# A cross-attention and mixture-of-experts block on one core: the second linear's ReLU values pass from ScalarE to VectorE as 16-bit integers instead of 32-bit floats

## What is computed

```python
def bitnet_linear(x, W, b):
    w_scale = jnp.maximum(jnp.mean(jnp.abs(W)), 1e-05)
    qW = jnp.sign(W) * (jnp.abs(W) > 0.5 * w_scale).astype(W.dtype)
    i_scale = jnp.maximum(jnp.max(jnp.abs(x)), 1e-08) / 127.0
    qx = jnp.clip(jnp.round(x / i_scale), -128.0, 127.0)
    out = jnp.einsum('...i,oi->...o', qx, qW) * (w_scale * i_scale)
    return out + b
...
h = jax.nn.relu(bitnet_linear(concatenated, W_f1, b_f1))   # 8192 tokens x 512
return bitnet_linear(h, W_f2, b_f2)                        # h is rounded to 0..127 first
```

## Time and profile before

| what | value |
|---|---|
| median of 3 runs | 553.0 us (550.98, 553.0, 557.37) |
| the profiled execution's own time | 551.12 us |
| its span in the trace | 549.3 us |
| busy over the span | PE 70%, DVE 69%, ACT 65%, POOL 36% |
| chain that ended last, by engine | PE 30%, DVE 24%, ACT 15%, issue 14%, POOL 13%, DMA 3% |
| line L759 (the ReLUs) in that chain | 2% as `xqT`, 2% as `tok_b` |

### The profile page before, as it was taken

How to read it: one execution, slowest core, us unless ns; L and a number is a source line. 1 busy time by engine, 2 the same in 40 slices (tenths; PEclk the granted TensorE clock), 3 DMA queues, 4 the chain that set the end, 5 groups by cost and what they waited for, 6 DMA issues and landing times.

```text
span 549.3 us, 10418 instructions
## 1 busy us (share of the span) xinstructions
PE 385.4 (70%) x2861; PEld 306.3 (56%) x2861; DVE 377.2 (69%) x941; ACT 355.8 (65%) x827; POOL 198.3 (36%) x276
## 2 busy tenths in 40 slices
PE   0370427999999789768784232154999988898994
PEld 0230015699989633335552222053999877787894
DVE  2999997578888779949998887893454443343452
ACT  1589987678888469769973541052877656566572
POOL 7300192253535200000000000006667777777764
PEclk9999999999999989978997555576999999999998
DMA  9920000000000000000339900005656555555550
GB/s 214 251 62 1 1 0 0 2 1 2 0 0 0 1 1 1 0 0 2 79 79 252 236 12 1 0 1 191 211 210 219 199 175 179 174 190 185 187 196 30
DMA packets 45137, 48.67 MB, mean 89 GB/s; under 512 B 10232, under 2 KB 32800, under 8 KB 45088
## 3 DMA queue, kind: packets, MB, share of 16 engines
q1 hardware_dynamic: 39728, 38.59, 23.4%
q0 software_dynamic: 4096, 8.46, 5.8%
q10 hardware_dynamic: 1264, 1.03, 0.7%
HBM read 16.20 MB, written 8.45 MB: 45 GB/s over the span
## 4 chain that ended last, share of the span: by engine, by line
PE 30%; DVE 24%; ACT 15%; issue 14%; POOL 13%; DMA 3%; SPq 0%; POOLq 0%; DVEq 0%; ACTq 0%
POOL out L594 9%; PE psum L956 6%; PE psum L972 5%; DVE big L1546 4%; POOL xall L587 4%; PE psum L1138 3%; ACT xqT L759 2%; PE psum L964 2%; PE psum L1147 2%; ACT tok_b L759 2%; DMA keys<-in_ctx 2%; ACT big L662 2%; DVE xqT L1628 2%; DVE part L1322 2%; ACT big L619 1%
## 5 line engine op out<-in xcount | busy, mean ns | idle before, releaser
L587 POOL DMA_INDIRECT xall<-token_rows,src_of x64 | 62.0, 968 | 201.2 <-DVE slot_of L1675 182.0
L828 ACT ACTIVATE xqT<-psum,feat 128x128 f32<-128x128 f32 x284 | 81.0, 368 | 39.2 <-PE psum L1138 38.2
L1147 PE MATMUL psum<-keys,xqT 128*128 x568 | 78.3, 281 | 1.5 <-issue 1.1
L1138 PE MATMUL psum<-xqT,feat 128*128 128x128 f32 x568 | 77.1, 280 | 0.0
L594 POOL DMA_INDIRECT out<-xall,src_of x64 | 63.2, 987 | 27.6 <-issue 16.8
L1147 PEld LDWEIGHTS psum<-keys,xqT 128*128 128x128 f32 x568 | 68.8, 192 | 5.6 <-issue 4.6
L1138 PEld LDWEIGHTS psum<-xqT,feat 128*128 128x128 f32 x568 | 70.8, 196 | 0.0
L1697 DVE TENSOR_SCALAR xqT<-xall 128x128 f32 x71 | 26.0, 366 | 41.2 <-DMA xall<-token_rows,src_of 39.7
L1703 DVE TENSOR_TENSOR xqT<-psum,feat 128x128 f32<-128x128 f32 x71 | 20.7, 292 | 44.2 <-PE psum L1147 35.4
L561 POOL TENSOR_TENSOR qb<-qb,arec 128x308 f32<-128x308 f32 x32 | 21.8, 699 | 64.6 <-DVE arec L1380 64.6
L972 PE MATMUL psum<-probT,keys 78*128 78x128 f32 x256 | 34.8, 282 | 1.8 <-ACT probT L724 1.8
(11 more groups left out here) (301 smaller groups left out, 927.9 us busy)
## 6 DMA issues: line engine op xcount, KB each, us to landing
feat<-keys SPq DMA_DIRECT2D x71, 322.0 KB
token_rows<-xall SPq DMA_DIRECT2D x4, 1040.0 KB, 8.0
xall<-in_x SPq DMA_DIRECT2D x8, 512.0 KB, 7.1
keys<-in_L_ffn_W SPq DMA_DIRECT2D x1, 2048.0 KB, 13.1
keys<-in_L_ffn_W SPq DMA_DIRECT2D x8, 256.0 KB, 6.6
keys<-in_ctx SPq DMA_DIRECT2D x4, 462.0 KB, 6.8
xall<-token_rows,src_of POOLq DMA_INDIRECT x64
out<-xall,src_of POOLq DMA_INDIRECT x64, 2.6
```

The costliest lines, as they stand in the source:

```text
L587: pool.indirect_dma_start(xring[:, t % RING, :], None, rows, bass.IndirectOffsetOnAxis(ap=src_of[:, t:t + 1], axis=0)).then_inc(s_g[t % TU ...
L828: m = act.activation(hT[a % DEPTH][:, P * c:P * c + P], bank(2 + a % 2)[:, P * c:P * c + P], ACT.Relu, bias=w_now[a % AHEAD][:, FF + c:FF ...
L1138: m = pe.matmul(bank(2 + a % 2)[:, P * c:P * c + P], w_now[a % AHEAD][:, P * c:P * c + P], gT[a % DEPTH], start=True, stop=True)
L1147: m = pe.matmul(bank(4 + a % 2, E), hT[a % DEPTH][:, P * c:P * c + P], w2s[:, bass.ds(e, 1), c, :].rearrange("p e d -> p (e d)"), start=(c ...
```

## The change

`u` is laid over the same memory, but as 16-bit integers: 4096 values of two bytes per partition instead of 4096 of four. ScalarE's ReLU instruction is otherwise as it was; its output type is now int16, so the conversion to an integer is made as ScalarE writes. VectorE's instruction, which added and subtracted the constant `MAGIC` to round a float and wrote bf16, is now a copy that converts int16 to bf16. Each engine has as many instructions as before, in the same order with the same waits; in VectorE's sequence the 11 instructions of L1464 read as CAST in place of TENSOR_SCALAR, and every other row of every engine is the same.

```diff
-        u = [v[:, :].bitcast(F32).rearrange("p (c n) -> p c n", c=NC) for v in (tok_b, xqT)]
+        u = [v[:, 0:NC * 2 * GT].bitcast(I16).rearrange("p (c n) -> p c n", c=NC) for v in (tok_b, xqT)]
         hq = [v[:, 0:NC * 2 * GT].rearrange("p (c n) -> p c n", c=NC) for v in (qa, qb)]
...
             def quantise_hidden(h):
                 wait(dve, s_f2, 2 * h - 2)
                 for c in range(0, NC, 1 if h == 0 else NC):
                     cs = slice(c, c + 1 if h == 0 else NC)
                     dve.wait_ge(s_relu, h * NC + cs.stop)
-                    m = dve.tensor_scalar(hq[h % 2][:, cs, :], u[h % 2][:, cs, :], MAGIC, MAGIC, ALU.add, ALU.subtract)
+                    m = dve.tensor_copy(hq[h % 2][:, cs, :], u[h % 2][:, cs, :])
                 m.then_inc(s_hq, 1)
```

## The result

The changed kernel takes 550.08 us in the median of 12 runs (548.61 to 553.45), against 553.0 before. The ratio of the two is 0.9951 with a 95% interval of 0.9931 to 0.9972, so 1.5 to 3.8 us are gained. The forecast was 550.0. The profiled execution took 549.54 us, with a span of 547.7.

A forecast was written before the change was run, and what follows sets the result against it. ScalarE was taken to bound the hidden stage. Second square root's wait 1.0 plus last conversion 1.07 gave 2.1 us, everything else 0; from 552.1, the middle of four times, the forecast was 550.0 us, range 546.4 to 554.2.

The forecast's parts named there:

- ScalarE sets the pace; faster conversions are hidden: Hidden stage, halves 1 to 6: 6.4 us come off VectorE, 0 on the path; its idle time grows to 9.6.
- The conversion's price: VectorE's int16-to-bf16 copy in SBUF: 4096 values fall from 2.29 to 1.22 us, 1024 values from 0.694 to 0.42.
- The two halvings: VectorE's conversion: a source in SBUF and 16-bit types each halve the time; combined, 4096 values take 1.22 us.
- ScalarE's price: ScalarE's 32 ReLUs: writing int16 instead of f32 changes their time by 0.
- The bounds of 1.15 and 2.6 us: Rivals at ScalarE's 32 ReLUs: int16 conversion costs up to 1.15 us (0.07), or narrower output gains up to 2.6 (0.04).
- The wait before the second square root: ScalarE's 1.08 us wait for the layer norm's `tmp` in the hidden stage: 1.0 us of it is gained.
- The last conversion: Hidden stage's end, no ReLUs left to hide behind: 2.29 to 1.22 us, wholly on the path, 1.07 us gained.
- The signs for this place: Stage's end: products after the last conversion start 2.1 us earlier, near 283.0, and the logits' copy L788 near 289.8.
- Everything behind shifts whole: Last products, routing and experts shift with their start, term 0; a change in routing's or experts' own length refutes the prediction.
- The rival of one value at a step: Conversion of 4096 takes 4.40 us, the bound moves to VectorE: +12.4 us, 564.5; chance 0.05.
- the threshold of 2.6 us: Conversion cost above which VectorE becomes the bound, 2.29 + 2.4 / 7; each further 0.1 us costs 0.7.
- The clock: Rival: TensorE's clock falls to half in the stage's last 6.8 us, some 4 us on top, about 554; chance 0.03.

The follow-up runs named there:

- all-but-last: Changed kernel with halves 0 to 6 as int16 and the last of the eight left f32; stage 52.64 us, ratio 0.9961 to the kernel before.
- the run in pieces: Whole change, with the last half converted chunk by chunk like the first; stage 51.65 us, ratio 0.9972 to the kernel before.
- its twin at full clock: Kernel with only the last half as int16, plus 12 unused matmuls filling TensorE's gap before the second half's products; stage 52.73 us, ratio 0.9978 to before.
- last half only: Only the last of eight halves written as int16 and converted by a copy, the others f32 as before; stage 54.06 us, ratio 0.9988 to before.
- the run at one value a step with the square roots moved: Whole change with scalar_tensor_tensor as conversion and ScalarE's square roots behind the two following ReLUs; stage 66.35 us, ratio 1.0213 to before.

## Why the prediction was right, point by point

- **The number.** The gain was forecast as 2.1 us and the stage lost 2.19. That the time itself came out at 550.08 us against 550.0 is in part luck: the forecast started at 552.1, the middle of four times, while the median of 12 runs is 553.0. From there the same sum gives 550.9, and the two medians lie 2.9 us apart, 0.7 more than the stage explains.
- **ScalarE sets the pace; faster conversions are hidden.** Right. Shown by all-but-last (six conversions worth one wait) and by VectorE's idle time before its large conversions, 10.2 us where 9.6 were forecast.
- **The conversion's price, 1.22 us.** Right: 1.226, and 0.428 for 1024 values. The two halvings that the rows showed one at a time do combine.
- **ScalarE's price, 0.** Right: 1.236 against 1.234 us. The bounds of 1.15 and 2.6 us were only bounds.
- **The wait before the second square root, 1.0 us.** Right in place and in size: the root starts 1.06 us sooner behind the copy ahead of it. From the first ReLU to the last it is 1.22; the other 0.15 is the clock's dip at 248 to 256 us, which I had left out. The f32 kernel with the root moved shows that the wait was worth its time by itself.
- **The last conversion, 1.07 us.** Right, 0.97 measured. The 0.1 that is missing is the start of TensorE's products, held up for 0.3 us by logits that wait for ScalarE's copy; in return TensorE runs them without a start gap. I had named nothing that is late next there. It was ScalarE's copy with the logit matmuls behind it, as the run in pieces shows. The signs for this place (products near 283.0, the logits' copy near 289.8) were given on the old clock; the whole stage starts 1.32 us later after the change. Counted from the first ReLU, the products start 2.0 us and the copy 2.19 us earlier.
- **Everything behind shifts whole.** Consistent with the ratio: 553.0 times 0.0049 is 2.7 us, with an interval of 1.5 to 3.8 that holds the 2.19. The routing kept its length, 80.8 us from the logits' copy to `slot_of` (L1675) in both. The experts' part was 0.8 us shorter, and by the letter of the prediction a change there was a sign against it; but the code is the same, and this part scatters by several us between executions, as told above. No cause in the change is shown for it, and the 1.32 ahead of the stage goes the other way.
- **The rival of one value at a step.** Right in kind, 2 us too low in the stage: I had counted VectorE's waits as slack, and the threshold of 2.6 us with it. Two of these waits, 1.7 us, are answers to VectorE's own delay, through the square root; the rest, 0.3 us, is a longer wait for TensorE's products at the low clock.
- **The clock.** I wrote that I saw no reason for another clock and priced it in the last stretch. It moves at the stage's start instead, and cost 1.3 us in one execution, against its twin at full clock. (The range was also said to leave this rival out; its price, 554, lies just inside 554.2.)

## What to carry to other kernels

Before a faster instruction is priced, find where its engine is waited for: here 11 conversions became faster by 8.5 us in all, and 2.2 us came of it, at one wait and at the stage's end. Look next for the same gain by order (one square root moved was worth as much as six conversions) and for work that fits into the idle time, which took another 7.5 us off the stage. And don't count a bounding engine's waits as slack before asking who held up the engine that it waits for.

## What the runs showed of the hardware

- VectorE copies int16 to bf16 in SBUF at 4096 values in 1.226 us, and applies two per-partition operands and a conversion to int16 to 1024 values in 0.494 to 0.53 us. A scalar_tensor_tensor over the same int16 values takes 4.41 us. The Trainium skill (VectorE: DVE Perf Modes, "The perf-mode tier table") lists four elements a cycle for copies and tensor_scalar on bf16 in SBUF. The copies of this case agree for int16: the ratio of 4.41 to 1.226 is 3.6, and 4.0 without the fixed 0.16 us that 4096 and 1024 values (1.226 and 0.428) give. The tensor_scalar with two per-partition operands lies above that rate, at 0.494 to 0.530 us against the copy's 0.428.
- The output's width made no difference to ScalarE (1.234 us writing f32, 1.236 writing int16).
- Behind a gap of 3.5 us at the stage's start TensorE's granted clock stood at 0.50 for some 6 us of work in one execution (last half only), for some 3 us in another (the kernel before, a mean of 0.71 from 252 to 256 us), and in the f32 kernel with the moved square root it stayed at 1.00. With the gap filled by matmuls it stayed at 1.00 in the one execution there is. With the shorter conversion the gap is 2.7 us; the clock stayed at 1.00 in the profiled executions of the change and of all-but-last, but had a mean of 0.71 from 248 to 252 us in that of the run in pieces, so the change doesn't protect from the dip.
- When the clock falls matters as much as whether it does. In the run at one value a step with the square roots moved, two gaps of 3.35 us were both followed by the low clock: behind the first the 16 products still took 1.07 us, behind the second 1.89. A gap of 2.6 us in the same execution was followed by none. What decides between such cases stays open.
